# Four gather rings of a graph network: POOL runs at most two groups ahead in place of four

## The chip, the cores and the metric

The kernel runs on one core of one Trainium2 chip, as one program. Its engines are PE (TensorE, matrix products and transposes), DVE (VectorE), ACT (ScalarE), POOL (GpSimd, here the engine that issues indirect DMAs) and SP (which only issues transfers). Each has its own instruction stream, and they meet through semaphores. The time is the device time of one execution in microseconds (us).

## What is computed

Four graph layers run one after the other on 50000 nodes with 128 features and 25000 edges sorted by target node; each is added to its input and normalised. Cut to its core:

```
edge_index = jnp.stack([src, dst])
x = _layernorm(x + _L0_gnn_ref(x, edge_index, edge_weight, ...))             # GIN, two convolutions
x = _layernorm(x + _L1_gnn_ref(x, edge_weight, bases, w_comp, src, dst, edge_type_8))   # relational
x = _layernorm(x + _L2_gnn_ref(x, L2_gnn_W, L2_gnn_bias, edge_index))        # GCN
x = _layernorm(x + _L3_gnn_ref(x, edge_index, edge_attr_128, ...))           # three attention layers

def _gin_conv(x, src, dst, wa, ba, wb, bb):
    agg = jax.ops.segment_sum(x[src], dst, num_segments=N_NODES)
    h = x + agg
    h = jnp.maximum(h @ wa + ba, 0.0)
    return h @ wb + bb
```

What matters here is `x[src]`: for each edge the row of its source node is fetched, and the rows of one target are summed.

## The kernel before

The 25000 edges stand in 197 chunks of 127 edges (one more slot of the 128 is kept free), four chunks to a group (`G4 = 4`), so 50 groups (`AG`). Four stages fetch the source rows of a group through a ring of `UN = 4` buffers, and do the same kind of work on each group:

- gin1 (`gin1_part`, in one block with the dense nodes' stage in front of it; the ring is `dg_g_ring`, gathers on line 732),
- gin2 (`phase_gin2`, ring `g_ring`, line 696),
- rgcn (`phase_rgcn`, ring `rg_ring`, line 696),
- gcn (`phase_gcn`, ring `gc_ring`, line 696).

In each, POOL issues for group i four indirect DMAs, one for a chunk, that write 128 rows into buffer i % 4. PE waits for all four and transposes them into PSUM (`g_p_t` on line 1144 for gin1 and on line 1379 for gin2, `rg_p_t` on line 1618, `gc_p_t` on line 1856); after the last of the four transposes the semaphore for the buffer goes up (`turned` in gin1, `pe_t` elsewhere). DVE then runs a scan over the 512 columns that sums the rows of each target (line 1230, 1519, 1943; rgcn does it by products with a selection matrix), and products, additions and a normalisation follow, several groups in flight on different engines. In gin1 DVE also copies a column of slot ids out of the ring (line 1238, `slot_id<-dg_g_ring`) after the scan of the group and the addition behind it, and raises `taken`. SP loads and stores the other tiles of a group (flags, edge attributes, old node rows, results) from its own queue.

The order of each engine is written out, group by group. POOL's own program in these stages is nothing but the gathers, so whatever it waits for holds up the later gathers of the same ring and nothing else; in gin1 the gathers of the dense part stand in front. The waits on POOL are:

- `gather_group` (gin2, rgcn, gcn): `wait(pool, freeing, i - UN + 1)`, where `freeing` counts transposed groups and `wait` leaves out a wait for zero or less; group i starts once groups 0 to i - 4 are transposed;
- `slot_gathers`, `rows(i)` (gin1): from group 4 on, the same for `turned` and for `taken`.

The blocks of the stages are separated by barriers: a stage begins when every engine is through with the one before. After gcn three attention layers follow (`phase_gats`), with no ring of this kind.

Of the kernel before, what the change touches and what calls it, by code (L numbers as in the profile page):

```python
# [40 lines left out]
FAR = 1 << 17  # L41
BIG = 1e30
UN = 4
FIRST = 24
EVERY = 5
PACE = 4
# [69 lines left out]
def steps(eng, count, lag, step, first=1):  # L116

    full = (count - 1) // UN  # L120
    for i in range(UN * first):
        step(i // UN, i % UN)
    with eng.Fori(first, full) as k:
        for u in range(UN):
            step(k, u)
    for i in range(full * UN, count + lag):
        step(i // UN, i % UN)

# [12 lines left out]
def wait(eng, sem, value):  # L141

    if not isinstance(value, int) or value > 0:
        eng.wait_ge(sem, value)
# [31 lines left out]
class Net:  # L176
# [293 lines left out]
    def segments_parts(self, sb, ps, sem):  # L470
# [152 lines left out]
        def gather_first(pool):  # L623
            nc.gpsimd.memset(self.msgs[:, USED:CHUNKS, :], 0.0).then_inc(padded, 1)
            pool.wait_ge(dst_ready, 1)
            self.resident_gather(self.dst_i, a["x"], D, self.got, range(FIRST))

# [62 lines left out]
    def gather_group(self, pool, i, idx, table, ring, width, arrived, freeing):  # L690


        u = i % UN
        wait(pool, freeing, i - UN + 1)
        for j in self.filled(i):
            self.nc.gpsimd.indirect_dma_start(  # L696
                out=ring[:, u, j, 0:width], out_offset=None, in_=table,
                in_offset=bass.IndirectOffsetOnAxis(ap=idx[:, i * G4 + j:i * G4 + j + 1], axis=0)).then_inc(arrived[u], 16)
# [9 lines left out]
    def slot_gathers(self, pool, ring, sem, arrived, turned, taken):  # L708


        nc, a = self.nc, self.a
        mapped = sem("g_mapped")
        begun = self.dense_begun
        done = [0]

        def after_ticks(ops):
            wait(pool, begun, min(done[0] // PACE + 1, DG))
            done[0] += ops

        def targets(chunks):  # L720
            for c in range(chunks.start, min(chunks.stop, USED), PACE):
                group = range(c, min(c + PACE, chunks.stop, USED))
                after_ticks(len(group))
                self.resident_gather(self.dst_i, a["x"], D, self.got, group)

        def rows(i):
            u = i % UN
            if i >= UN:
                pool.wait_ge(turned, i - UN + 1)
                pool.wait_ge(taken, i - UN + 1)  # L730
            for j in self.filled(i):
                nc.gpsimd.indirect_dma_start(  # L732
                    out=ring[:, u, j, :], out_offset=None, in_=self.xw,
                    in_offset=bass.IndirectOffsetOnAxis(ap=self.src_i[:, i * G4 + j:i * G4 + j + 1], axis=0)).then_inc(arrived[u], 16)

        targets(range(FIRST, FIRST + EVERY * COPIES))
        pool.wait_ge(self.x_copied, 16 * COPIES)
        for c in range(USED):
            if c % PACE == 0:
                after_ticks(min(PACE, USED - c))  # L740
            nc.gpsimd.indirect_dma_start(  # L741
                out=self.places, out_offset=bass.IndirectOffsetOnAxis(ap=self.put_i[:, c:c + 1], axis=0),
                in_=self.slot_id[:, c:c + 1], in_offset=None).then_inc(mapped, 16)
        targets(range(FIRST + EVERY * COPIES, CHUNKS))
        pool.wait_ge(mapped, 16 * USED)
        for i in range(AG):
            rows(i)
# [1930 lines left out]
```

## Time and profile before

| | us |
|---|---|
| median of 3 runs | 3409.42 (3407.78 to 3427.02) |
| profiled execution | 3423.15 |
| its span, first to last instruction | 3421.2 |

The page of the profile gives for each engine the busy time, and the span in 40 slices of 85.5 us. A digit is the busy share of a slice in tenths; PEclk is the granted TensorE clock in tenths of full speed.

```profile
## 1 busy us (share of the span) xinstructions
PE 2864.1 (84%) x18099; PEld 2324.5 (68%) x18099; DVE 2636.8 (77%) x8154; ACT 2242.8 (66%) x5891; POOL 1954.8 (57%) x1994
## 2 busy tenths in 40 slices
PE   4889999969979997886676799988999887886886
...
POOL 6656666527747756762776366603565036644776
PEclk8999999978969998998688798979998889777555
DMA  6997666746744553554677588856898568776553
```

The four stages with rings lie in the slices 9 to 22 (about 739 to 1880 us). Every group of gathers has one line in the page's list of costliest groups: line, engine, operation, output and inputs, count, then busy time with the mean of one in ns, and the idle time of the engine just before, with what ended most of it.

```profile
L732 POOL DMA_INDIRECT dg_g_ring<-t_xw,src_i x197 | 192.4, 977 | 129.3 <-DVE slot_id L1238 76.0
...
L696 POOL DMA_INDIRECT gc_ring<-t_x,row_i x197 | 192.0, 974 | 117.0 <-issue 59.7
L696 POOL DMA_INDIRECT rg_ring<-t_x,row_i x197 | 197.6, 1003 | 106.3 <-issue 52.1
...
L696 POOL DMA_INDIRECT g_ring<-t_h,row_i x197 | 197.0, 1000 | 93.4 <-issue 59.4
```

In a timeline a row is: start, duration, engine, line, operation, output<-inputs, shapes, count, and in brackets the idle time of the engine before it and what ended it ("issue": nothing that the profile shows).

### The profile page before, as it was taken

The numbers are of one execution on the slowest core, as the hardware profiler recorded it, in microseconds if no ns is written. First come the engines' busy times: TensorE is split into PE (matmuls) and PEld (weight loads), VectorE is DVE, ScalarE is ACT, GpSimd is POOL, SyncE is SP. The second block draws the span as 40 slices with busy tenths as digits, with TensorE's granted clock in tenths as the row PEclk, the third lists the DMA queues.
The fourth block names the chain that finished last, engine by engine and source line by source line (L and its number), as shares of the span: only waits on it lengthen the run. The fifth ranks groups of instructions, "written<-read, shape, count | busy, mean of one in ns | idle before, by whom it ended". The sixth has DMA issues, their size and how long they took to land. (4 is left out here: it accounts for less than half of the span.)

```text
span 3421.2 us, 67477 instructions
## 1 busy us (share of the span) xinstructions
PE 2864.1 (84%) x18099; PEld 2324.5 (68%) x18099; DVE 2636.8 (77%) x8154; ACT 2242.8 (66%) x5891; POOL 1954.8 (57%) x1994
## 2 busy tenths in 40 slices
PE   4889999969979997886676799988999887886886
PEld 3667777745536553453566799988999776776885
DVE  5989999975648876997677357866487888988996
ACT  2888888832215555887466567866587777776885
POOL 6656666527747756762776366603565036644776
PEclk8999999978969998998688798979998889777555
DMA  6997666746744553554677588856898568776553
GB/s 216 398 333 236 221 222 224 258 146 197 216 131 127 148 142 119 184 178 154 187 231 229 174 271 289 273 162 222 254 297 256 184 220 267 249 221 194 150 171 107
DMA packets 419338, 723.50 MB, mean 211 GB/s; under 512 B 76431, under 2 KB 137908, under 8 KB 418606
## 3 DMA queue, kind: packets, MB, share of 16 engines
q1 hardware_dynamic: 350990, 610.53, 53.5%
q0 software_dynamic: 63040, 107.35, 12.3%
q10 hardware_dynamic: 5024, 2.30, 0.3%
q8 instruction: 122, 2.00, 0.3%
q14 instruction: 162, 1.33, 0.1%
HBM read 428.65 MB, written 321.10 MB: 219 GB/s over the span
## 5 line engine op out<-in xcount | busy, mean ns | idle before, releaser
L704 POOL DMA_INDIRECT msgs<-t_gat,row_i x591 | 577.8, 978 | 667.6 <-PE t_p_nt L2128 254.0
L2291 ACT ACTIVATE t_nnt<-t_p_nt,cxt 128x512 f32<-128x512 f32 x294 | 200.3, 681 | 221.1 <-PE t_p_nt L2128 220.9
L1774 PEld LDWEIGHTS t_p_q<-mean_col,t_nsq 128*128 128x128 f32 x2352 | 334.8, 219 | 12.9 <-issue 12.6
L1774 PE MATMUL t_p_q<-mean_col,t_nsq 128*128 128x1 f32 x2352 | 324.0, 259 | 9.5 <-ACT t_asd L2326 7.4
L2128 PE MATMUL t_p_nt<-ident,t_nh 128*128 128x128 f32 x1176 | 211.7, 310 | 82.8 <-ACT t_nsq L2292 55.7
L741 POOL DMA_INDIRECT t_xw<-slot_id,put_i x197 | 199.7, 1014 | 122.0 <-PE de_p_a L891 73.9
L732 POOL DMA_INDIRECT dg_g_ring<-t_xw,src_i x197 | 192.4, 977 | 129.3 <-DVE slot_id L1238 76.0
L704 POOL DMA_INDIRECT msgs<-in_x,dst_i x197 | 196.0, 995 | 119.5 <-PE de_p_a L891 58.7
L696 POOL DMA_INDIRECT gc_ring<-t_x,row_i x197 | 192.0, 974 | 117.0 <-issue 59.7
L696 POOL DMA_INDIRECT rg_ring<-t_x,row_i x197 | 197.6, 1003 | 106.3 <-issue 52.1
L1767 PE MATMUL t_p_nh<-wx,t_nnt 128*128 128x132 f32 x1568 | 251.1, 309 | 1.9 <-DVE t_hn L1788 1.5
L2051 POOL DMA_INDIRECT out_rows<-t_hn,own_i x197 | 194.8, 989 | 97.8 <-issue 60.3
L696 POOL DMA_INDIRECT g_ring<-t_h,row_i x197 | 197.0, 1000 | 93.4 <-issue 59.4
L1599 PE MATMUL rg_p_b<-bases,rg_gt 128*128 128x512 f32 x400 | 200.9, 606 | 30.6 <-DVE rg_mg L1717 30.6
L2128 PEld LDWEIGHTS t_p_nt<-ident,t_nh 128*128 128x128 f32 x1176 | 152.6, 159 | 101.9 <-issue 65.4
L1767 PEld LDWEIGHTS t_p_nh<-wx,t_nnt 128*128 128x128 f32 x1568 | 216.1, 211 | 2.3 <-issue 1.9
L863 PE MATMUL de_p_o<-wc,de_hh 128*128 128x128 f32 x1568 | 210.1, 277 | 7.2 <-DVE de_r L990 7.2
L863 PEld LDWEIGHTS de_p_o<-wc,de_hh 128*128 128x128 f32 x1568 | 193.0, 191 | 26.2 <-DVE de_r L990 11.9
L1788 DVE TENSOR_TENSOR t_hn<-t_p_nh,t_ninv 128x264 f32<-128x264 f32 x392 | 151.3, 427 | 65.7 <-PE t_p_nh L1767 62.1
L1717 DVE SCALAR_TENSOR_TENSOR rg_mg<-rg_p_b,coef,rg_mg 128x128 f32<-128x128 f32 x600 | 177.2, 343 | 30.5 <-ACT rg_mg L1652 25.8
L2292 ACT ACTIVATE t_nsq<-t_p_nt,cxt 128x512 f32<-128x512 f32 x294 | 199.8, 679 | 0.0
L1774 PEld LDWEIGHTS t_p_q<-mean_col,t_asq 128*128 128x128 f32 x1200 | 190.5, 241 | 0.8 <-issue 0.6
(411 smaller groups left out, 8103.0 us busy)
## 6 DMA issues: line engine op xcount, KB each, us to landing
t_gat<-t_hn SPq DMA_DIRECT2D x296, 264.0 KB
t_nh<-t_gat SPq DMA_DIRECT2D x294, 264.0 KB
t_x<-de_x SPq DMA_DIRECT2D x196, 256.0 KB
t_ah<-t_gat SPq DMA_DIRECT2D x150, 264.0 KB
t_gat<-de_h SPq DMA_DIRECT2D x98, 264.0 KB
t_xw<-in_x_map SPq DMA_DIRECT2D x28, 903.0 KB
de_xt<-in_x_t SPq DMA_DIRECT2D x98, 256.0 KB
t_xn<-t_x SPq DMA_DIRECT2D x98, 256.0 KB
```

The costliest lines, as they stand in the source:

```text
L696: self.nc.gpsimd.indirect_dma_start(out=ring[:, u, j, 0:width], out_offset=None, in_=table, in_offset=bass.IndirectOffsetOnAxis(ap=idx[:, ...
L704: self.nc.gpsimd.indirect_dma_start(out=self.msgs[:, c, 0:width], out_offset=None, in_=table, in_offset=bass.IndirectOffsetOnAxis(ap=idx[: ...
L732: nc.gpsimd.indirect_dma_start(out=ring[:, u, j, :], out_offset=None, in_=self.xw, in_offset=bass.IndirectOffsetOnAxis(ap=self.src_i[:, i ...
L741: nc.gpsimd.indirect_dma_start(out=self.places, out_offset=bass.IndirectOffsetOnAxis(ap=self.put_i[:, c:c + 1], axis=0), in_=self.slot_id[ ...
L863: m = nc.tensor.matmul(p_o[:, j * D:(j + 1) * D], hh[:, u % 2, t, j * D:(j + 1) * D], self.wc[:, t, :], start=(t == 0), stop=(t == 1))
L1599: nc.tensor.matmul(p_b[j][:], gt[:, (u - 1) % 2, j * D:(j + 1) * D], self.bases[:].rearrange("i b o -> i (b o)"), start=True, stop=True).t ...
L1767: last = self.nc.tensor.matmul(p_h[:, j // 2, (j % 2) * XW:(j % 2 + 1) * XW], xt[:, j * D:(j + 1) * D], self.wx[:, layer, :], start=True, ...
L1774: last = self.nc.tensor.matmul(p_q[:, j:j + 1], sq[:, j * D:(j + 1) * D], self.mean_col[:], start=True, stop=True)
L2051: nc.gpsimd.indirect_dma_start(out=self.out, out_offset=bass.IndirectOffsetOnAxis(ap=self.own_i[:, c:c + 1], axis=0), in_=held[:, item % X ...
L2128: t = nc.tensor.transpose(p_nt[:, j * D:(j + 1) * D], nh[:, g % NR, j, 0:D], self.ident[:])
L2291: nc.scalar.activation(nnt[:, g % 2], p_nt[:], ACT.Identity, bias=bias).then_inc(act_nt, 1)
L2292: nc.scalar.activation(nsq[:, g % 2], p_nt[:], ACT.Square, bias=bias).then_inc(act_nq, 1)
```

## The change

A constant `AHEAD = 2` is added, and the three waits on POOL use it in place of `UN`. The rings keep their four buffers, and a group still goes to buffer i % 4. Group i now starts once groups 0 to i - 2 are transposed (and, in gin1, their slot ids copied). In `gather_group` that gives groups 2 and 3 a wait that they did not have; in `rows(i)` the condition `i >= UN` stays, so that gin1's first four groups still go without a wait, and group 4 is the first that waits, for three groups done in place of one.

```diff
--- before.py
+++ after.py
@@ -41,6 +41,7 @@
 FAR = 1 << 17
 BIG = 1e30
 UN = 4
+AHEAD = 2
 FIRST = 24
 EVERY = 5
 PACE = 4
@@ -691,7 +692,7 @@
 
 
         u = i % UN
-        wait(pool, freeing, i - UN + 1)
+        wait(pool, freeing, i - AHEAD + 1)
         for j in self.filled(i):
             self.nc.gpsimd.indirect_dma_start(
                 out=ring[:, u, j, 0:width], out_offset=None, in_=table,
@@ -726,8 +727,8 @@
         def rows(i):
             u = i % UN
             if i >= UN:
-                pool.wait_ge(turned, i - UN + 1)
-                pool.wait_ge(taken, i - UN + 1)
+                pool.wait_ge(turned, i - AHEAD + 1)
+                pool.wait_ge(taken, i - AHEAD + 1)
             for j in self.filled(i):
                 nc.gpsimd.indirect_dma_start(
                     out=ring[:, u, j, :], out_offset=None, in_=self.xw,
```

No instruction changes its place among those that do work. The one thing that moves in POOL's order is where the first wait of a stage stands. At the start of gin2 (g_ring is the ring, t_h the table that is read) POOL has, before:

```order
L696 DMA g_ring<-t_h,row_i 128x64 x16
L696 DMA g_ring<-t_h,row_i 128x64 [waits st_told]
L696 DMA g_ring<-t_h,row_i 128x64 x3
L696 DMA g_ring<-t_h,row_i 128x64 [waits st_told]
L696 DMA g_ring<-t_h,row_i 128x64 x3
```

and after (the line number is one higher for the constant that was added):

```order
L697 DMA g_ring<-t_h,row_i 128x64 x8
L697 DMA g_ring<-t_h,row_i 128x64 [waits st_told]
L697 DMA g_ring<-t_h,row_i 128x64 x3
L697 DMA g_ring<-t_h,row_i 128x64 [waits st_told]
L697 DMA g_ring<-t_h,row_i 128x64 x3
```

The name in brackets is that of the semaphore's first user; here it is the count of transposed groups. Sixteen gathers went without a wait, now eight do; from there on the first gather of each group waits, as before, for a count that is now two higher.

## Rows read from the trace of the kernel before

**Rows 1.** the engines in each stretch: busy us, TensorE clock, share of the DMA engines.

```profile
core 0: us, PE busy (x) PEld busy (x) DVE busy (x) ACT busy (x) POOL busy (x), PEclk, DMA share, GB/s
...
783.00:834.00 51.00, 50.69 (x205) 25.28 (x202) 27.70 (x53) 10.23 (x17) 38.80 (x41) 0.74 0.65 187
834.00:903.00 69.00, 67.55 (x358) 37.54 (x358) 44.43 (x90) 18.85 (x30) 52.77 (x54) 0.99 0.73 221
903.00:985.00 82.00, 81.05 (x361) 42.05 (x361) 46.35 (x90) 18.85 (x30) 51.34 (x53) 0.83 0.62 183
1004.00:1042.00 38.00, 21.94 (x62) 12.01 (x63) 10.83 (x20) 3.63 (x6) 29.04 (x30) 0.53 0.35 91
...
1101.00:1270.00 169.00, 159.34 (x801) 97.99 (x800) 138.91 (x469) 97.85 (x229) 122.65 (x123) 1.00 0.54 151
...
1620.00:1880.00 260.00, 169.53 (x1112) 159.64 (x1112) 176.09 (x378) 147.63 (x440) 191.97 (x197) 0.80 0.71 214
```

**Rows 2.** POOL's waits, 738 to 1880 us: total us, times, longest us.

```profile
POOL dg_g_ring L732 <- DVE slot_id L1238: 76.0, 22, 69.6
...
POOL rg_ring L696 <- PE rg_p_t L1618: 20.8, 25, 1.1
...
POOL g_ring L696 <- PE g_p_t L1379: 0.3, 1, 0.3
```

**Rows 3.** timeline, start of gin1's ring: start us, us, engine, line, operation, [idle before].

```profile
738.94 0.94 POOL L732 DMA_INDIRECT dg_g_ring<-t_xw,src_i  x1 [69.58 <-DVE slot_id L1238]
...
744.37 0.16 DVE L1238 COPY slot_id<-dg_g_ring 128x4 f32<-128x4 f32 x1
...
750.51 0.64 PE L1144 MATMUL g_p_t<-ident,dg_g_ring 128*128 128x128 f32 x4
```

**Rows 4.** timeline, gin1 where PE waits for a gather.

```profile
778.58 0.66 PE L1144 MATMUL g_p_t<-ident,dg_g_ring 128*128 128x128 f32 x4 [0.72 <-DMA dg_g_ring<-t_xw,src_i]
779.06 0.94 POOL L732 DMA_INDIRECT dg_g_ring<-t_xw,src_i  x1 [0.30 <-issue]
...
781.05 0.19 DVE L1238 COPY slot_id<-dg_g_ring 128x4 f32 x1
...
783.51 1.11 PE L1144 MATMUL g_p_t<-ident,dg_g_ring 128*128 128x128 f32 x4 [0.31 <-DMA dg_g_ring<-t_xw,src_i]
```

**Rows 5.** gin1's transposes, three stretches: count, ns min/median/max, first and last start.

```profile
L1144 PE MATMUL g_p_t<-ident,dg_g_ring x52: 272/273/328, 837.0 to 892.0; 128*128 128x128 f32 x52
...
L1144 PE MATMUL g_p_t<-ident,dg_g_ring x36: 272/310/478, 783.5 to 831.3; 128*128 128x128 f32 x36
...
L1144 PE MATMUL g_p_t<-ident,dg_g_ring x184: 272/273/478, 750.5 to 984.5; 128*128 128x128 f32 x184
```

**Rows 6.** gin2: its start in the timeline, then its transposes and gathers, 1101 to 1270.

```profile
1035.70 1.06 PE L1379 MATMUL g_p_t<-ident,g_ring 128*64 128x128 f32 x4
...
1039.78 0.94 POOL L696 DMA_INDIRECT g_ring<-t_h,row_i  x1 [0.30 <-issue]
...
1042.25 0.60 PE L1379 MATMUL g_p_t<-ident,g_ring 128*64 128x128 f32 x4
...
L1379 PE MATMUL g_p_t<-ident,g_ring x132: 270/272/302, 1101.2 to 1268.1; 128*64 128x128 f32 x132
L696 POOL DMA_INDIRECT g_ring<-t_h,row_i x123: 940/945/1447, 1100.6 to 1259.9; - x123
```

**Rows 7.** timeline, rgcn in the steady part.

```profile
1456.28 0.60 PE L1618 MATMUL rg_p_t<-ident,rg_ring 128*128 128x128 f32 x4
...
1457.15 1.26 POOL L696 DMA_INDIRECT rg_ring<-t_x,row_i  x1 [0.89 <-PE rg_p_t L1618]
...
1462.17 0.60 PE L1618 MATMUL rg_p_t<-ident,rg_ring 128*128 128x128 f32 x4
```

**Rows 8.** timeline, gcn, the tightest place.

```profile
1798.56 1.09 PE L1856 MATMUL gc_p_t<-ident,gc_ring 128*128 128x128 f32 x4 [3.30 <-issue]
...
1800.65 0.94 POOL L696 DMA_INDIRECT gc_ring<-t_x,row_i  x1 [0.30 <-issue]
```

## The prediction

> **What bounds the kernel now.** I read the page first: PE is busy 84% of the span, DVE 77%, POOL 57%. None of these says what a gather that starts later costs, so the reading goes stage by stage. Four stages read through a ring of four buffers: gin1 (the `dg_g_ring` gathers, about 739 to 985 us of the span), gin2 (1004 to 1268), rgcn (1294 to 1587) and gcn (1622 to 1878). The busy times by stretch [rows 1] show the TensorE clock as well: in gin1 it is 1.00 or 0.99 in some stretches and 0.74 or 0.83 in others (a mix of the two levels, 1.2 and 2.4 GHz), in the steady part of gin2 1.00, in gcn 0.80.
>
> The second view is POOL's waits [rows 2]. Where POOL waits for the ring now, the line names slot_id (gin1) or p_t (the others); "issue" with 0.3 us is only the gap between two gathers. In gin1 POOL waits 76.0 us for slot_id, but 69.6 of them are one wait at the start of the ring. In rgcn it waits 25 times for the transposes; in gin2 once, 0.3 us; for gcn's transposes there is no such line. So in gin1, gin2 and gcn POOL issues gather after gather at 0.94 + 0.30 = 1.24 us with an occasional longer one, and is itself the pace: gin2's POOL row gives (1259.9 - 1100.6) / 122 = 1.306 us a gather, 5.22 us a group of four, and its transposes take (1268.1 - 0.4 - 1101.2) / 32 = 5.20 us a group [rows 6]. (0.4 is the time from the first to the last transpose of a group; the trace has 33 groups of transposes there.) In rgcn a group takes 5.89 us (1462.17 - 1456.28) and POOL waits [rows 7].
>
> gin1 is the interesting one. At the full clock a group of transposes follows the last after (891.6 - 837.0) / 12 = 4.55 us, faster than POOL's 5.0; in the stretch of clock 0.74 after (831.3 - 0.4 - 783.5) / 8 = 5.93 us, slower than POOL; over the 45 steps from group 4 to group 49 (184 transposes, four a group) after (984.5 - 0.4 - 750.5) / 45 = 5.19 us [rows 5]. That mean is POOL's pace. The four buffers are what makes it so: while PE is slow POOL runs ahead, and while PE is fast it lives on that lead.
>
> **What the change does.** No operation is added or removed. Group i of a ring may be issued once group i-2 is transposed, in place of group i-4; in gin1 the copy of its slot ids by DVE must be done as well. Behind the waiting POOL instruction stand only the later gathers of the same ring, and PE's transposes wait for those; SP's and ACT's transfers are on other queues and never behind it. What is late after a stall is the group's arrival, then the transposes, then DVE's scan of that group.
>
> The new loop is: transposes of i-2 start, buffer freed, four gathers, landing, transposes of i start; two groups fit in it. Its parts for gin1 come from one group that PE had to wait for [rows 4]. Transposes start at 778.58, the copy of slot ids ends at 781.05 + 0.19 = 781.24: 2.66 us. From the release to the gather takes 0.27 us, read in rgcn where POOL waits every time: the transposes end at 1456.28 + 0.60 = 1456.88, the gather starts at 1457.15, and that first gather is 1.26 us long, not 0.94 [rows 7]. Four gathers then take 1.26 + 3 x 1.25 = 5.01 us. From the end of the last gather (779.06 + 0.94 = 780.00) to the transposes at 783.51 it is 3.51 us [rows 4]. Sum: 2.66 + 0.27 + 5.01 + 3.51 = 11.45 us for two groups, 5.73 us a group.
>
> The Trainium skill's page "DMA: Bandwidth & Descriptors" (section "Anatomy of one DMA — SWDGE (gpsimd) path") prices one such DMA at 2.0 us plus bytes / 436e3. For a gather of 128 x 129 floats that is an estimate of 2.15 us from its start, where rows 4 show 4.45 (783.51 - 779.06); by the page the loop would be 9.15 us, POOL's own pace would hold, and gin1 would lose next to nothing. The trace does not agree, since the gathers here share the DMA engines with SP's loads, and I go by the row.
>
> **gin1, step by step.** (a) The start. POOL now starts group 4 at 738.94 after the copy of group 0; it must wait for the copy of group 2, which ends at 744.37 + 0.16 = 744.53 [rows 3]. Its transposes then start at 744.53 + 0.27 + 5.01 + 3.51 = 753.3 in place of 750.51 [rows 3]. (b) The pace. At the full clock 5.73. Where the clock is at its low level PE takes longer than the loop by itself: with x the share of the low level the stretch of clock 0.74 gave 5.93 with x = 0.52, and it contains groups of 4.55, which the loop no longer allows. Now 5.73 is above what PE needs at the full clock (4.55), so PE idles about a fifth of each step, and the clock fell in just those stretches where PE had begun to wait for gathers (0.74 from 783 on, behind the wait in rows 4). I take 5.8 as the mean, between 5.73 and 5.93. The ends: 5.4, when the landing is 2.9 us rather than 3.5 (2.66 + 0.27 + 5.01 + 2.9 = 10.8), which is also POOL's own pace when each group begins with the long gather (5.01 + 0.27, plus the odd long one); and 6.1: the slow stretch's 5.93 mixes slow steps with fast ones, which can't be under 5.4 any more; if a quarter of its steps took 4.55, they add 0.85 / 4 = 0.2. (c) The last group is then at 753.3 + 45 x 5.8 = 1014.3 in place of 984.1: +30 us. The ends: +12 (5.4) and +44 (6.1).
>
> **gin2.** The slack in the steady part: a loop without the copy is 0.60 + 0.27 + 5.01 + about 3.5 = 9.4 us for two groups against 2 x 5.20, so nothing is lost there. But the stage begins at clock 0.53 with one long step: group 4's transposes start at 1035.70, group 5's at 1042.25 and end 0.60 later [rows 6]. POOL passed this without waiting; its group 7 started at 1039.78. It will have to wait for 1042.85 + 0.27: 3.3 us late. Since POOL is the pace from about group 17 on and never waits [rows 2], what it loses once is not recovered: +3.3 us, and at least 2, since PE may give up some of its margin; group 6 is part of the same delay.
>
> **rgcn and gcn.** In rgcn the step of 5.89 us is set by DVE and PE; the loop of 0.60 + 0.27 + 5.01 + 3.5 = 9.4 us is shorter than 2 x 5.89 = 11.8: 0. If that cover were gone it would cost what the loop exceeds two steps. In gcn POOL is the pace, and the transposes of i-2 are over before group i starts: in the tightest place I found the transposes end at 1798.56 + 1.09 = 1799.65 and POOL starts the group after next at 1800.65, 1.0 us later, of which the release takes 0.27 [rows 8]. So 0, up to +2 if the clock (0.80 there) puts a slow step in a worse place. The stages behind, the long attention stage included, are untouched.
>
> **Sum.** 30 + 3 + 0 + 0 = +33 us. The profiled execution has a span of 3421.2 us and took 3423.15; that becomes 3456. The median of the three runs shown is 3409.42, 14 us lower, and the prediction is given on that: 3409.4 + 33 = 3442.4, **3442 us**, 1.0% slower.
>
> **The rivals.**
> B, the ring of two is nearly enough. For it: only 0.54 us per group (5.73 against 5.19) stands between loss and none, and the 3.5 us of landing were measured while PE, SP and POOL all hurried at once; a longer step leaves SP's loads more time. Against it: the start (a) and gin2 lose anyway. It gives 5.4 us a group or less: 3409.4 + 12 + 3, or less with a pace of 5.3 (+7 and +2): 3418 to 3424. The Trainium skill ("Trainium Kernel Development and Optimization", section "Best Practices") says to double-buffer so that DMA and compute overlap; taken at its word, two groups suffice and nothing changes.
> C, the clock stays low through most of gin1. For it: 0.74 and 0.83 where PE waits. Against: 0.99 for 69 us on end now. From 4.55 at 1.00 to 5.93 at 0.74 is 0.053 us per hundredth; at clock 0.65 that makes 6.4 us a group, +57 with the start, and +3: 3469 and beyond if lower. The skill's page "TensorE: Matmul & The Clock Gate" (section "HAM oscillation — how this bites in real kernels") describes this: a wait for a DMA in every pass drops the clock in every pass. In gcn, where PE waits in every group, the trace shows 0.80 and not the low level throughout.
> D, faster. With fewer gathers in flight they and SP's loads may land sooner in gin1, and PE keeps the full clock. At a landing of 2.1 us in place of 3.5 the loop is 10.0 us, 5.0 us a group, which is as fast as POOL can issue: 45 x 0.19 = 8.5 us saved, less 1.4 at the start (744.53 + 0.27 + 5.01 + 2.1 = 751.9 for 750.51) and 3 in gin2: 4 us faster, 3405. It turns into a gain only below 5.09 us a group (0.1 us a group pays the 4.4), and over 1% is out of its reach. E, the new wait never binds: rows 3 exclude it for group 4 alone.
>
> **Chances.** Forecast (5.6 to 6.0 us a group, +24 to +42 in all) 0.55; B 0.25; C 0.15; D with E 0.05. A measurement of this kernel can tell about 1% (34 us) from no change; that line lies at 5.82 us a group, so all of C and half of the forecast are beyond it: slower 0.42, same 0.55, faster 0.03. The range leaves out D and B's lowest end below and the larger part of C above: 3418 to 3465.
>
> **What would show it.** Right: POOL's waits in gin1 with some 40 entries for slot_id, not 22; PE waiting for `dg_g_ring`; gin1's transposes 5.6 to 6.0 us apart, last ones near 1014 on the old time scale; its clock lower over the stage; gin2 with one or two waits of POOL for g_p_t and 3 us longer; rgcn and gcn with the lengths of before, rgcn with twice the wait per group hidden. Wrong: gin1 no longer than before (the landing is shorter than 3.5), or gcn or the steady part of gin2 longer (POOL waits there each group: the margin of 1 us was not one).

## The result, and the profile after

| | before, us | changed, us |
|---|---|---|
| median of the runs | 3416.2 (3407.8 to 3427.0, 4 runs) | 3484.5 (3469.3 to 3500.9, 4 runs) |
| span of the profiled execution | 3421.2 | 3467.3 |

The ratio is 1.020, with a 95% interval of 1.016 to 1.024: slower by 2.0%, twice the 1.0% that was forecast, and above the top of the range (3465).

On the page of the changed kernel the busy times of DVE, ACT and POOL are within 3 us of those of before. PE's is 22.7 us longer (2886.8 for 2864.1) with the same 18099 instructions, and POOL's idle time before gin1's gathers is 193.1 us, where it was 129.3.

```profile
PE 2886.8 (83%) x18099; PEld 2326.6 (67%) x18099; DVE 2638.4 (76%) x8154; ACT 2243.4 (65%) x5891; POOL 1951.8 (56%) x1994
...
PEclk7999999967877998999689898989999889678555
...
L733 POOL DMA_INDIRECT dg_g_ring<-t_xw,src_i x197 | 188.6, 957 | 193.1 <-DVE slot_id L1239 141.9
```

In POOL's waits from 738 to 1940 us (total, times, longest), gin1's wait for the slot ids has 40 entries in place of 22, and the longest is longer by 6.3 us. The other 21 of before were 0.3 us each, the gap that every gather has; the other 39 here are 1.7 us in the mean. rgcn's wait has 40 entries in place of 25, gin2's two in place of one [rows 2].

```profile
POOL dg_g_ring L733 <- DVE slot_id L1239: 141.9, 40, 75.9
...
POOL rg_ring L697 <- PE rg_p_t L1619: 35.3, 40, 1.1
...
POOL g_ring L697 <- PE g_p_t L1380: 3.2, 2, 2.7
```

The transposes of gin1, groups 4 to 49: the first transpose of group 49 starts at 1041.0, 0.7 us before its last, so the step is (1041.0 - 756.0) / 45 = 6.33 us a group where it was 5.19 [rows 5].

```profile
L1145 PE MATMUL g_p_t<-ident,dg_g_ring x184: 272/328/477, 756.0 to 1041.7; 128*128 128x128 f32 x184
```

The busy times by stretch, for this part of gin1 and for everything behind gcn (stretch, its length, busy us of PE, PEld, DVE, ACT, POOL with counts; then TensorE clock, share of the DMA engines, GB/s):

```profile
core 0: us, PE busy (x) PEld busy (x) DVE busy (x) ACT busy (x) POOL busy (x), PEclk, DMA share, GB/s
756.00:1041.00 285.00, 262.71 (x1081) 135.22 (x1081) 140.31 (x270) 56.54 (x90) 166.21 (x174) 0.78 0.57 163
1936.90:3467.30 1530.40, 1306.14 (x9224) 1245.69 (x9222) 1173.14 (x3366) 1093.91 (x2782) 773.68 (x788) 0.81 0.70 222
```

The clock over this part is 0.78. In the kernel before it is 0.88:

```profile
750.50:984.10 233.60, 230.17 (x1083) 121.78 (x1082) 138.78 (x270) 57.02 (x91) 167.73 (x172) 0.88 0.67 200
```

These two rows say what the 51.4 us between 233.6 and 285.0 are made of. PE is busy 32.5 us longer (262.7 for 230.2) with the same instructions, which is the lower clock, and it stands still for 22.3 us in place of 3.4, which is 18.9 more. Standing still is all waiting for gathers: PE's waits in this part (total, times, longest), before and after:

```profile
PE g_p_t L1144 <- DMA dg_g_ring<-t_xw,src_i: 3.4, 5, 1.4
...
PE g_p_t L1145 <- DMA dg_g_ring<-t_xw,src_i: 22.3, 21, 2.6
```

So PE waits for the gathers in 21 of 46 groups and not in the others. The two kinds follow each other. Groups 11, 12 and 13 of the changed kernel:

```profile
799.63 1.12 PE L1145 MATMUL g_p_t<-ident,dg_g_ring 128*128 128x128 f32 x4 [0.88 <-DMA dg_g_ring<-t_xw,src_i]
...
807.93 1.11 PE L1145 MATMUL g_p_t<-ident,dg_g_ring 128*128 128x128 f32 x4
...
814.64 0.66 PE L1145 MATMUL g_p_t<-ident,dg_g_ring 128*128 128x128 f32 x4
```

Group 11 has waited 0.88 us. The step behind it takes 8.3 us without any wait, at the low level (0.50) throughout; the next takes 6.7 us, also without a wait, at 0.65.

Read stage by stage in the two traces: gin1's last transposes end at 984.8 before and at 1042.2 after, +57.4 us, of which 1.6 lie ahead of its first group. From gin2's first gather to its last transposes it is 264.3 and 265.2 us, for rgcn 292.5 and 292.8, for gcn 256.2 and 256.7. Behind gcn it is 1543.0 and 1530.4. So the changed kernel's loss is gin1's. The stages behind differ by themselves: in the fourteen traces of this study this part took 1521 to 1568 us, with no order by kernel. Here it was 12.6 us shorter after the change, so the two profiled spans are 46 us apart and not 58; the 68 us between the medians have an interval of 55 to 82. Below, a stage's own length is therefore read beside the time of a run.

One pass of the loop in the changed kernel, in the timeline of gin1:

```profile
872.11 0.66 PE L1145 MATMUL g_p_t<-ident,dg_g_ring 128*128 128x128 f32 x4 [1.33 <-DMA dg_g_ring<-t_xw,src_i]
...
874.59 0.16 DVE L1239 COPY slot_id<-dg_g_ring 128x4 f32 x1
...
875.50 0.94 POOL L733 DMA_INDIRECT dg_g_ring<-t_xw,src_i  x1 [0.81 <-DVE slot_id L1239]
...
879.25 0.95 POOL L733 DMA_INDIRECT dg_g_ring<-t_xw,src_i  x1 [0.30 <-issue]
...
883.29 0.65 PE L1145 MATMUL g_p_t<-ident,dg_g_ring 128*128 128x128 f32 x4
```

The transposes start at 872.11 and the copy of the slot ids ends at 874.75; the first gather of the group after next starts at 875.50, 0.75 us later; the last of its four gathers ends at 880.20, and the transposes start at 883.29. That is 11.18 us for two groups, at the full clock. PE did not wait for the second of them (its row has no bracket). This is a good pass; the mean is 12.57.

### The profile page after: what moved, and what is told of

Its sections match the earlier page's. It is cut to its first block and busy times, and to the rows that moved or that the text cites. A ratio compares the mean times of both kernels' runs of the same rounds, so it can differ in the third digit from the quotient of the medians.

```text
span 3467.3 us, 67477 instructions
## 1 busy us (share of the span) xinstructions
PE 2886.8 (83%) x18099; PEld 2326.6 (67%) x18099; DVE 2638.4 (76%) x8154; ACT 2243.4 (65%) x5891; POOL 1951.8 (56%) x1994
## 5 line engine op out<-in xcount | busy, mean ns | idle before, releaser
L733 POOL DMA_INDIRECT dg_g_ring<-t_xw,src_i x197 | 188.6, 957 | 193.1 <-DVE slot_id L1239 141.9
L1768 PE MATMUL t_p_nh<-wx,t_nnt 128*128 128x132 f32 x1568 | 244.1, 303 | 2.2 <-DVE t_hn L1789 1.5
L1183 ACT ACTIVATE g_ha<-g_p_a,b1a 64x512 f32<-64x512 f32 x50 | 34.1, 682 | 273.0 <-PE g_p_b L1159 245.8
## 6 DMA issues: line engine op xcount, KB each, us to landing
t_gat<-t_hn SPq DMA_DIRECT2D x296, 264.0 KB
t_nh<-t_gat SPq DMA_DIRECT2D x294, 264.0 KB
t_ah<-t_gat SPq DMA_DIRECT2D x150, 264.0 KB
t_gat<-de_h SPq DMA_DIRECT2D x98, 264.0 KB
```

Of the source, the lines that this page charges most:

```text
L733: nc.gpsimd.indirect_dma_start(out=ring[:, u, j, :], out_offset=None, in_=self.xw, in_offset=bass.IndirectOffsetOnAxis(ap=self.src_i[:, i ...
L1768: last = self.nc.tensor.matmul(p_h[:, j // 2, (j % 2) * XW:(j % 2 + 1) * XW], xt[:, j * D:(j + 1) * D], self.wx[:, layer, :], start=True, ...
```

## The experiments

For each kernel the step of gin1 and the loop's parts are worked out from its trace in one way, in us: step and clock from group 4 to group 49, the parts as means over groups 6 to 48. "Copy" runs from the start of the transposes to the end of the copy of slot ids, "release" from there to the first gather of the group after next (negative where this gather starts before the copy has ended), "gathers" to the end of the fourth, "landing" from there to the start of its transposes. The four add up to two steps by their definition, in every kernel, whether or not the loop holds anything up; and "landing" holds, besides the transfer, the time in which PE is not ready yet. The last two columns say how long PE was busy and how long it stood still between groups 4 and 49; they add up to 45 steps. There is one trace of each kernel.

| kernel | time to before | 95% interval | step | clock in gin1 | copy | release | gathers | landing | PE busy | PE still |
|---|---|---|---|---|---|---|---|---|---|---|
| before | | | 5.19 | 0.88 | 3.08 | -3.86 | 4.81 | 6.26 | 230.2 | 3.4 |
| changed | 1.0201 | 1.0160 to 1.0241 | 6.33 | 0.78 | 3.05 | 0.82 | 4.78 | 3.92 | 262.7 | 22.3 |
| gin1 alone two ahead | 1.0147 | 1.0084 to 1.0209 | 6.29 | 0.79 | 3.04 | 0.82 | 4.78 | 3.94 | 259.4 | 23.7 |
| the other three two ahead | 1.0007 | 0.9976 to 1.0039 | 5.15 | 0.89 | 3.10 | -4.68 | 4.82 | 7.12 | 227.9 | 3.9 |
| gin1 two ahead, copy four | 1.0052 | 1.0024 to 1.0080 | 5.26 | 0.89 | 3.05 | -1.47 | 4.79 | 4.17 | 229.0 | 7.5 |
| gin1 three ahead | 1.0007 | 0.9984 to 1.0031 | 5.28 | 0.89 | 3.05 | -2.71 | 4.82 | 5.43 | 228.0 | 9.8 |
| gin1 two ahead, PE filled | 1.0186 | 1.0136 to 1.0236 | 6.47 | 0.85 | 2.93 | 0.83 | 4.80 | 4.43 | 274.5 | 16.7 |
| gin1 two ahead, copy early | 1.0118 | 1.0072 to 1.0164 | 6.06 | 0.82 | 2.45 | 0.88 | 4.76 | 4.05 | 247.8 | 24.9 |
| gin1 two ahead, no attribute loads | 1.0164 | 1.0112 to 1.0216 | 5.98 | 0.83 | 3.03 | 0.85 | 4.78 | 3.43 | 246.4 | 22.9 |
| gin1 two ahead, one wait | 1.0146 | 1.0110 to 1.0183 | 6.26 | 0.77 | 3.10 | 0.36 | 4.73 | 4.32 | 264.0 | 17.6 |
| one wait and copy early | 1.0090 | 1.0059 to 1.0121 | 5.75 | 0.85 | 2.40 | 0.47 | 4.82 | 3.81 | 241.8 | 17.1 |
| ring of six, six ahead | 0.9965 | 0.9942 to 0.9987 | 4.92 | 0.93 | 2.99 | -6.35 | 4.88 | 8.21 | 218.6 | 3.0 |
| ring of seven, seven ahead | 0.9968 | 0.9942 to 0.9993 | 4.73 | 0.97 | 2.97 | -10.19 | 4.87 | 11.79 | 211.2 | 1.6 |
| ring of six, four ahead | 0.9982 | 0.9956 to 1.0008 | 5.10 | 0.90 | 2.99 | -4.75 | 4.82 | 7.10 | 225.5 | 3.9 |

The step is uncertain by itself: single steps run from 4.5 to 9.6 us, with a standard deviation of 0.8 to 1.0 (0.5 with seven buffers), so a mean over 45 of them is uncertain by 0.12 to 0.15 us, and a difference of two such means by about 0.2.

### Which ring costs it

The change in gin1 alone, with the others back at four:

```diff
 def gather_group(...):
-        wait(pool, freeing, i - AHEAD + 1)
+        wait(pool, freeing, i - UN + 1)
```

> Two ahead in gin1 alone, four ahead in gin2, rgcn and gcn. Theory G (the loss is made in gin1): gin1's transposes stay 6.3 us apart as in the changed kernel, and the time is 45 to 70 us above the kernel before. Theory O (the loss comes as much from the other rings or from how they meet the stages behind): less than 25 us above it.

Measured: 1.0147 to the kernel before, 50 to 55 us more. Its transposes, groups 4 to 49; the first ones of the two start at 755.4 and 1038.5:

```profile
L1145 PE MATMUL g_p_t<-ident,dg_g_ring x184: 272/328/476, 755.4 to 1039.2; 128*128 128x128 f32 x184
```

That is (1038.5 - 755.4) / 45 = 6.29 us, the changed kernel's step. The ratio is lower than the changed kernel's 1.0201, but the two intervals overlap. And the other way round, the change in the other three rings alone (shown against the changed kernel):

```diff
 def rows(i):
-                pool.wait_ge(turned, i - AHEAD + 1)
-                pool.wait_ge(taken, i - AHEAD + 1)
+                pool.wait_ge(turned, i - UN + 1)
+                pool.wait_ge(taken, i - UN + 1)
```

> Two ahead in gin2, rgcn and gcn, four ahead in gin1. Theory G: within 5 us of the kernel before, gin2 one to three us longer, rgcn and gcn the same. Theory O: 25 us or more above the kernel before.

Measured: 1.0007, no difference. The two together hold theory G: the loss is made in gin1. gin2 took 262.3 us in this trace, where the kernel before shows 264.3 and the other traces 260.3 to 265.4, so its expected 1 to 3 us are below what a trace can tell.

### Which wait, and how short a lead is enough

gin1 two ahead by the transposes only; the copy's wait stays at four:

```diff
                 pool.wait_ge(turned, i - AHEAD + 1)
-                pool.wait_ge(taken, i - AHEAD + 1)
+                pool.wait_ge(taken, i - UN + 1)
```

> gin1 alone two ahead, but only by the wait for the transposes; the wait for DVE's copy of the slot ids is four ahead as before. Theory C (the copy is the long part of the loop, 2.7 us after the transposes start and more at the low clock): the loop falls by about 2 us for two groups, gin1's step to 5.2 to 5.5 us, the time to 5 to 20 us above the kernel before. Theory K (the step is set by the low TensorE clock once PE waits at all, however short the loop): the step stays above 6.0 and the time 40 us or more above.

Measured: 1.0052, 16 us between the medians. The transposes start at 750.3 and, for group 49, at 986.8: a step of 5.26.

```profile
L1145 PE MATMUL g_p_t<-ident,dg_g_ring x184: 272/273/473, 750.3 to 987.2; 128*128 128x128 f32 x184
```

So theory K falls: by the transposes the lead is two groups here as well, and PE waits in ten groups, but for 7.5 us in all; the clock is 0.89, the step near that of before. What was taken out of the loop is the time from the end of the transposes to the end of the copy. Where POOL waits for PE here, it starts 0.27 us after the transposes' end (876.88 + 0.66 = 877.54, then 877.81):

```profile
876.88 0.66 PE L1145 MATMUL g_p_t<-ident,dg_g_ring 128*128 128x128 f32 x4
...
877.81 0.94 POOL L733 DMA_INDIRECT dg_g_ring<-t_xw,src_i  x1 [1.11 <-PE g_p_t L1145]
```

The 16 us of the medians are more than the 3 us by which gin1 is longer in this trace; the part behind gcn happened to be the longest of all here (1568.4 us at clock 0.78, against 1521.2 at 0.81 in the trace with the other rings two ahead). Whether other executions lose more in gin1 is not shown.

```profile
1878.90:3447.30 1568.40, 1351.49 (x9224) 1292.46 (x9222) 1172.46 (x3365) 1097.93 (x2780) 775.52 (x788) 0.78 0.69 216
```

```profile
1871.70:3392.90 1521.20, 1296.69 (x9224) 1238.07 (x9222) 1173.52 (x3366) 1092.07 (x2782) 772.27 (x788) 0.81 0.71 223
```

Three ahead in gin1, both waits (shown against the kernel with gin1 two ahead):

```diff
-AHEAD = 2
+AHEAD = 3
```

> gin1 alone three ahead, both waits. Three groups in a loop of 11.6 us need 3.9 us each, so in the steady state it does not bind. Theory C: the time is within 8 us of the kernel before, since only the lead for slow stretches is smaller. Theory K (any loss of lead brings more waiting and more of the low clock): 15 to 40 us above it, a step of 5.5 to 6.0.

Measured: 1.0007, no difference, and a step of 5.28:

```profile
L1145 PE MATMUL g_p_t<-ident,dg_g_ring x184: 272/273/478, 751.1 to 989.2; 128*128 128x128 f32 x184
```

A loop of 11 to 12.6 us holds three groups at 3.7 to 4.2 us each, less than POOL's own 5.0. With two it is 5.5 to 6.3, more. The cost begins between two and three.

### The parts of the loop

PE kept busy before it waits (six transposes of the identity into a bank of its own, ahead of the transposes of each group from group 7 on):

```diff
+FILL = 6
...
                     if live(k, u, 1, AG):
+                        for j in range(FILL if i >= 8 else 0):
+                            nc.tensor.transpose(p_f[:, 0:128], self.ident[:], self.ident[:])
                         pe.wait_ge(arrived[v], ...)
```

> gin1 alone two ahead, and from group 8 on PE makes six transposes more (of the identity into a PSUM bank that nobody reads, about 0.9 us at the full clock) before it waits for a group's gathers. Theory L (the loop by itself, 2.7 + 0.7 + 4.7 + 3.5 = 11.6 us for two groups, sets 5.8 us and the low TensorE clock adds the rest up to 6.1 to 6.3): with PE kept busy the clock in gin1 rises from 0.75 to above 0.9 and the step falls to 5.8 to 5.9, 10 to 20 us less than the same without the fill. Theory M (the low clock adds nothing, the loop is simply longer than read): the step stays at 6.1 or rises by part of the 0.9 us.

Measured: 1.0186, and the step did not fall but is 6.47. The clock did rise, to 0.85:

```profile
751.10:1042.30 291.20, 274.53 (x1340) 159.18 (x1340) 142.74 (x272) 57.05 (x91) 168.62 (x176) 0.85 0.59 161
```

The fill itself, in the groups by line of the same stretch (operation, count, then busy us and mean ns):

```profile
L1144 PE MATMUL g_p_f<-ident 128*128 128x128 f32 x258 | 44.7, 319 | 0.0
```

Theory L's step did not come, and its clock came only in part. The clock's share shows all the same, in PE's busy time. Beside it the kernel with gin1 two ahead and no fill:

```profile
755.40:1038.50 283.10, 259.36 (x1082) 134.38 (x1082) 140.81 (x270) 57.08 (x91) 168.22 (x176) 0.79 0.58 165
```

Without the records of the fill PE is busy 237.9 us here, against 259.4: PE's own work got 21.5 us shorter with the higher clock, and it stood still 7.0 us less. But the fill added 274.5 - 237.9 = 36.6 us of busy time (its row has 44.7, part of which overlaps PE's own work), since it runs in every group, also in those where PE has nothing to wait for. The sum is 8 us longer. So the step of 6.47 is not a sign that the clock costs nothing; the fill costs more than the clock gives back. A fill in the waiting groups alone was not run.

The copy ahead of the addition on DVE:

```diff
+                    if live(k, u, 1, AG):
+                        ... nc.vector.tensor_copy(self.slot_id[...], xs[:, v, :, D]) ...
                     if live(k, u, 2, AG):
                         ... nc.vector.tensor_tensor(xb[:, u % 2], self.msgs[...], ..., ALU.add) ...
-                    if live(k, u, 1, AG):
-                        ... nc.vector.tensor_copy(self.slot_id[...], xs[:, v, :, D]) ...
```

> gin1 alone two ahead, with DVE's copy of the slot ids ahead of the addition of 0.67 us (xb) that stood in front of it. Theory L: the loop is 0.67 us shorter for two groups, the step 0.33 shorter, 15 us or a little more gained on the kernel with gin1 two ahead. Theory T (the copy is not in the loop; the wait for the transposes is): no gain.

Measured: the copy ends 2.45 us after the transposes start and not 3.04, and the step is 6.06, 0.23 shorter, 10 us over the 45 steps, where 15 were expected. That is hardly more than the uncertainty of the difference, and the time of 1.0118 has an interval that overlaps that of gin1 two ahead, so this run alone doesn't decide. Theory T falls by the kernel above in which only the copy's wait was put back to four: its step went from 6.29 to 5.26.

No attribute loads after the fourth group. The attention terms of the later edges are left out by this, and so is SP's wait in front of those loads:

```diff
-                        wait(sp, s["pe_r"], i - UN + 1)
-                        sp.dma_start(tr[:, u], a["attr_t"][...]).then_inc(arrivede[u], 16)
+                        if isinstance(i, int) and i < UN:
+                            sp.dma_start(tr[:, u], a["attr_t"][...]).then_inc(arrivede[u], 16)
```

> gin1 alone two ahead, and SP loads the edge attributes (256 KB a group) for the first four groups only; the later groups use stale ones, so the attention terms of the edges are left out. Theory L (3.5 us from the last gather's end to the transposes is mostly sharing the DMA engines with SP's loads): the landing falls to 2.5 or less, the step to 5.3 to 5.7, 20 us or more gained on the kernel with gin1 two ahead. Rival: the landing is a gather's own time, it stays at 3.3 to 3.5, and less than 8 us are gained.

Measured: the landing is 3.43 us in the mean, not 3.94; the step 5.98, 14 us over the stage. That lies between the two expectations. Over the groups for which PE waited, 22 in each trace, the landing is 2.74 us, not 3.24: without SP's loads of `tr` it is half a microsecond shorter, and 2.7 us remain. The time, 1.0164, does not show the 14 us; with an interval of 1.0112 to 1.0216 it doesn't exclude them.

POOL waiting for the copy only, which comes after the transposes anyway (shown against the kernel with gin1 two ahead):

```diff
-                pool.wait_ge(turned, i - AHEAD + 1)
                 pool.wait_ge(taken, i - AHEAD + 1)
```

> gin1 alone two ahead, and POOL waits only for the copy of the slot ids; the wait for the transposes in front of it is taken out, since the copy comes after them anyway. With both waits the gather started 0.75 us after the copy's end, where rgcn shows 0.27 after PE's transposes. Theory W (two waits in a row cost the half microsecond): release 0.27, step 0.24 shorter than 6.3. Theory V (a release by DVE takes 0.75, one by PE 0.27): release still 0.75, step unchanged within 0.1.

Measured: theory W on the release. The copy ends at 885.92 + 0.17 = 886.09, the gather starts at 886.36, 0.27 us later:

```profile
885.92 0.17 DVE L1238 COPY slot_id<-dg_g_ring 128x4 f32 x1
...
886.36 0.94 POOL L732 DMA_INDIRECT dg_g_ring<-t_xw,src_i  x1 [1.09 <-DVE slot_id L1238]
```

In the changed kernel it is 0.75 (once 0.76) after 39 of the 40 such waits. So it is not that DVE raised it: with the other wait taken out, POOL starts 0.48 us sooner after the same copy. Two waits in the code are not enough for the 0.75, though. In the kernel with the copy's wait at four both waits stand, the first is the one that POOL is held by, and it starts 0.27 us after it. The 0.75 was seen only where the second of the two came last.

But the step went down by 0.03 only, and the time not at all. PE stood still 6.1 us less than with both waits (17.6 for 23.7) and was busy 4.6 us more (264.0 for 259.4), at a clock of 0.77:

```profile
755.30:1036.90 281.60, 264.00 (x1080) 136.16 (x1080) 139.10 (x268) 56.49 (x90) 165.80 (x174) 0.77 0.57 164
```

Both, one wait and the early copy:

> The same with DVE's copy moved ahead of the addition too. If the loop's parts add up (copy's end 3.05 us after the transposes start, release 0.82, four gathers 4.78, landing and start 3.92, together 12.57 for two groups), this one has 2.45 + 0.27 or 0.75 + 4.78 + 3.9 = 11.4 or 11.9 us, a step of 5.7 or 5.95, 15 to 27 us less than with gin1 two ahead. If the time is set elsewhere (low clock), the step stays at 6.1 or more.

Measured: 2.40 + 0.47 + 4.82 + 3.81 = 11.50 us for two groups, a step of 5.75, 24 us less between groups 4 and 49 than with gin1 two ahead:

```profile
L1144 PE MATMUL g_p_t<-ident,dg_g_ring x184: 272/273/476, 751.7 to 1011.0; 128*128 128x128 f32 x184
```

The time is 1.0090. The 11.50 is the value that the expectation had from the sum of the parts (11.4). Of the 24 us 6.6 are PE standing still less, and 17.6 are PE's busy time, 241.8 for 259.4 at a clock of 0.85 without any fill. So a shorter loop is paid back mostly as clock. The 0.03 for one wait alone and the 0.24 that was expected of it are not far apart beside the 0.2 by which such a difference is uncertain.

### More buffers

If a short lead costs, a longer one might pay: before gin1 POOL stands for 70 us with its ring full [rows 3].

```diff
+RING = 6
 def rows(i):
-            u = i % UN
-            if i >= UN:
-                pool.wait_ge(turned, i - UN + 1)
-                pool.wait_ge(taken, i - UN + 1)
+            u = i % RING
+            if i >= RING:
+                pool.wait_ge(turned, i - RING + 1)
+                pool.wait_ge(taken, i - RING + 1)
...
-            rs2 = sb("rs2", [128, UN, G4])
+            rs2 = self.coef[:, 0, 0:UN * G4].rearrange("p (u g) -> p u g", u=UN)
...
-            ring = sb("g_ring", [128, UN, G4, MW])
+            ring = sb("g_ring", [128, RING, G4, MW])
```

> The kernel before with six buffers in gin1's ring and six ahead (a small tile of the dense part shares memory with another to make room; DVE's loop in gin1 is written out). POOL stands for 70 us before gin1 with its ring full. Theory P (gin1 is paced by POOL, and every group that is fetched before it starts is a group less): two groups of 5.1 us, 8 to 12 us less than the kernel before. Rival (the lead only smooths, the pace is PE's mean with the low clock): no difference within 4 us.

Measured: 0.9965 (0.9942 to 0.9987), 12 us faster than the kernel before. The step of gin1 is (971.0 - 749.4) / 45 = 4.92:

```profile
L1146 PE MATMUL g_p_t<-ident,dg_g_ring x184: 272/273/477, 749.4 to 971.3; 128*128 128x128 f32 x184
```

```profile
749.40:971.00 221.60, 218.56 (x1082) 118.66 (x1082) 137.31 (x270) 57.03 (x91) 161.03 (x163) 0.93 0.72 207
```

Theory P in size. Where the 12.0 us come from is another matter: PE stood still 3.4 us before and 3.0 here, and its busy time fell from 230.2 to 218.6, with the clock at 0.93 where it was 0.88. The kernels with six and seven buffers also have DVE's loop written out; that alone was not run, but the last kernel of this part has it too and gained next to nothing. Seven buffers (the tile h1 of the dense part moved into `coef`, rs2 into `et_c`):

> The kernel before with seven buffers and seven ahead in gin1 (another tile of the dense part shares memory). Six gave 12 us less than before, with gin1's mean clock 0.93 and 36 of 45 steps at 4.5 us. Theory P (each group fetched ahead of the start saves POOL's 5.1 us until PE's own 4.55 a group is the bound, (4.92 - 4.55) x 45 = 17 us away): 3 to 5 us less than with six. Rival: six is enough, no difference beyond 2 us.

Measured: 0.9968 (0.9942 to 0.9993). In the trace the last group's transposes start at 966.5, 4.5 us before those of six, as theory P has it, and the step is 4.73 at clock 0.97, with PE busy 211.2 us. The block began later in this trace; counted from gin1's first transposes it is 9.0 us between the two and not 4.5:

```profile
L1146 PE MATMUL g_p_t<-ident,dg_g_ring x184: 272/273/429, 753.7 to 966.9; 128*128 128x128 f32 x184
```

The times of six and seven, each against its own runs of the kernel before, do not tell the two apart. At last, six buffers, the first six groups without a wait, and four ahead from there:

> Six buffers in gin1, the first six groups without a wait, from group 6 on only four ahead. Theory S (the gain of six buffers is what is fetched before the stage begins): group 6 waits for group 2 and starts at about 745 in place of 749 in the kernel before, so 4 to 5 us less than before. Theory D (the gain is the deeper lead, which carries PE over slow stretches and keeps its clock up): 2 us or less, and the clock in gin1 falls back to 0.88.

Measured: 0.9982 (0.9956 to 1.0008), which excludes neither theory. Its one trace is of the longest of its twelve executions (3442 us, the median is 3411), so it decides nothing either: the clock is 0.90 and group 49 starts at 983.4, where kernels with gin1's ring as it was have 984.1 and 982.6. Whether the gain of six buffers is the early fetch or the deeper lead stays open.

## Why the prediction failed, point by point

**What bounds the kernel.** Right: gin1 is where the ring's depth matters, and the other three rings can do with two. The experiments that split the change show it. One reading was half of it: the 5.19 us were called POOL's pace, but in that trace PE is busy 230.2 of 233.6 us, so they are just as much PE's own pace at a mean clock of 0.88.

**(a) The start of gin1.** Predicted: group 4's gathers released by the copy of group 2, transposes at 753.3. In the changed trace:

```profile
745.96 0.16 DVE L1239 COPY slot_id<-dg_g_ring 128x4 f32<-128x4 f32 x1
...
746.87 0.94 POOL L733 DMA_INDIRECT dg_g_ring<-t_xw,src_i  x1 [75.90 <-DVE slot_id L1239]
```

Released by the copy, after a wait 6.3 us longer than before, transposes at 756.0. The release is as forecast; that the transposes are late for it is not shown. They have no wait for gathers in this trace:

```profile
748.44 1.09 PE L1145 MATMUL g_p_t<-ident,dg_g_ring 128*128 128x128 f32 x4
...
756.04 1.09 PE L1145 MATMUL g_p_t<-ident,dg_g_ring 128*128 128x128 f32 x4
```

PE was at the low level for the whole of groups 2 to 4. From gin1's first transposes to those of group 4 it is 38.1 us here and 34.2 before, but 36.4 in the trace in which gin1 has its old lead. The forecast's 2.8 us lie within that spread, and of the 5.5 us that were measured 1.6 are a later start of the whole block.

**(b) The pace. This is the step that failed.** It was put at 5.8 us a group: 5.73 where the clock is full, by the loop, 5.93 where it is low, by PE. The changed kernel's 45 steps fall into 14 at clock 1.00, 5.70 us in the mean, and 31 below it, 6.62 us in the mean at a clock of 0.70. So the first value held and the second was too low, and most of the steps are of the second kind. The 5.93 was the mean of a stretch of before that held steps of 4.55 as well; the range's upper end, 6.1, allowed for a quarter of such steps. In the changed kernel nine steps at a clock of 0.72 took 6.1 us without any wait, and five at 0.50 took 8.3. The prediction also had PE idle for a fifth of each step; it was idle for 8% of the time (22.3 of 285.0), because it was slow for much of the rest. In sum: 0.72 us a group more of PE's busy time and 0.42 more of waiting, 1.14 in all, where 0.6 was forecast.

The loop's own terms were off by less. For the 21 groups that PE waited for, and only there does the sum measure the loop: the copy's end 3.08 for 2.66; the release 0.75 for 0.27; four gathers 4.84 for 5.01; landing 3.20 for 3.51. Together 11.87 for 11.45, 0.2 us a group, 9 us over the stage. Two of the four are too low and two too high, so part of the agreement is luck. The other 22 of the 43 loops took 13.25 us for two groups, with PE not waiting at their end and a clock of 0.72. The copy was read from one pass, in which PE had just waited for its gathers; the mean over the stage in the trace of before was already 3.08. The release was read in rgcn, on a single wait, though gin1 has two waits in a row; its own value stood in the rows: the copy of group 0 ends at 738.19 and the gather it released starts at 738.94 [rows 3].

**The clock.** It fell in gin1 from 0.88 to 0.78. The forecast had it lower, without a number and with next to no price. Rival C had the size right (6.4 us a group, +57 us) and the larger part of the cause, but not its measure: it had a clock of 0.65, and at its own rate of 0.053 us per hundredth the 0.78 gives only 5.7 us. The rest is the waiting, which comes on top. That waiting lowers the clock is shown as far as this: the kernels in which PE stood still for 16 to 25 us have 0.77 to 0.85, those with 2 to 10 us have 0.88 to 0.97, and the fill raised it from 0.79 to 0.85. Each is one trace.

**(c) and the sum.** Group 49 is 57 us later (1041.0 for 984.1), where 30 was forecast: 51.4 from the pace, 5.5 from the start. The medians are 68 apart with an interval of 55 to 82, so gin1 alone is enough for the loss. The range came out too low because the pace's upper end of 6.1 was.

**gin2.** The wait came where it was put: group 7 starts 0.27 us after the transposes of group 5.

```profile
1093.30 1.06 PE L1380 MATMUL g_p_t<-ident,g_ring 128*64 128x128 f32 x4
...
1094.64 0.94 POOL L697 DMA_INDIRECT g_ring<-t_h,row_i  x1 [2.67 <-PE g_p_t L1380]
...
1099.30 0.60 PE L1380 MATMUL g_p_t<-ident,g_ring 128*64 128x128 f32 x4
...
1100.17 0.94 POOL L697 DMA_INDIRECT g_ring<-t_h,row_i  x1 [0.58 <-PE g_p_t L1380]
```

The transposes of group 5 end at 1099.90, the gather starts at 1100.17; with the wait of the group before it POOL lost (2.67 - 0.30) + (0.58 - 0.30) = 2.7 us. Counted from the stage's first gather, group 7 starts 2.9 us later than before, near the 3.3 forecast, and groups 20 and 30 2.3 us later; but group 40 is only 0.9 late, the stage as a whole 0.9 us longer, and not longer with the other three alone. So what POOL lost was not kept to the end, as the prediction had it. The gathers' own durations take back 2.0 us here: those that are longer than the usual 0.94 exceed it by 9.0 us in all, where it was 11.0. With 260.3 to 265.4 us for the stage in all traces, that may be chance.

**rgcn and gcn.** Right: 292.5 and 292.8 us, 256.2 and 256.7. In rgcn POOL waits oftener (40 entries for 25), and the stage is no longer for it.

**The rivals.** B (two is enough, as "double-buffer" would have it) is wrong for gin1 and right for the other three: what decides is whether two steps are longer than the loop. What a loop that is too long costs is then the waiting and the clock together. The price of the Trainium skill's page "DMA: Bandwidth & Descriptors" (section "Anatomy of one DMA — SWDGE (gpsimd) path"), 2.0 us plus bytes / 436e3, an estimate of 2.15 us, was too low here: for the 21 groups that PE waited for it is 0.94 + 3.20 = 4.14 us in the mean from the last gather's start to the transposes, and never below 3.2. D is excluded.

## What to carry to other kernels

A ring needs at least as many groups in flight as one step of the slowest engine goes into the loop (free, issue, land, use), rounded up. Here the loop was 11 to 12.6 us and POOL's step 5.0, so three were enough and two cost 2% of the kernel. With fewer, the price is not the loop's excess alone. PE's own work got slower between the waits, and that was 32.5 of the 51.4 us; so count PE's busy time before and after, and take the price of a low clock from steps that are wholly slow, not from a mixed stretch. Read the loop's terms from the passes in which the consumer waited, more than one of them, and the release from a place with the same waits. A buffer's second use (here a column of ids copied late in DVE's order) belongs to the loop as well: with its wait put back to four the step was 5.26, with one more group in flight 5.28.

## What the runs showed of the hardware

- With two waits in a row on POOL, the gather starts 0.75 us after the event when the second wait is the one that ends last, and 0.27 us after it when the first is. With one wait it is 0.27, whether PE or DVE raised it.
- An indirect gather of 128 rows of 516 bytes costs POOL 0.94 + 0.30 us when nothing disturbs it. The first gather behind a wait took 0.94 us in the changed kernel, 1.14 with one wait and the early copy, and 1.26 in the place read in rgcn.
- One group of gin1 takes PE 4.55 us at clock 1.00, 6.14 at 0.72 and 8.30 at 0.50, with no wait in it. Of the 51.4 us that the changed kernel's groups 4 to 49 are longer, 32.5 are this.
- Six transposes of no use a group raised gin1's granted clock from 0.79 to 0.85 and shortened PE's own work by 21.5 us; they took 36.6 us themselves, and the stage was longer.
- The part behind gcn, whose code no kernel here changes, took 1521 to 1568 us in fourteen traces (clock 0.81 and 0.78 at the ends), 1.4% of the span; that hides anything smaller in one profiled span.
